# Adaptive layer-norm block on one core: the attention's output projection as two float32r matmuls on split operands, with the order of all steps remade

## The reference

```
h = layernorm(x) * (1 + ca) + sa
x = x + ga * attention(h)          # 16 query heads summed to 4, d = 16, rope, causal softmax
h = layernorm(x) * (1 + cb) + sb
x = x + gb * ffn(h)                # router; rmsnorm, wv, wo; rmsnorm, w_gate, w_up (704), w_down
```

## Time and profile before

| | us |
|---|---|
| median of 3 runs | 510.67 (510.49 to 515.2) |
| profiled execution, its own time | 510.83 |
| its span, first to last instruction | 509.1 |
| PE / PEld busy | 453.8 / 376.4 |
| DVE busy | 363.1 |
| ACT busy | 283.4 |
| POOL busy | 256.9 |

### The profile page before, as it was taken

The page is one execution under the profiler, slowest core; times in us unless marked ns, Lnnn a source line. Parts: engine busy times, 40 slices in busy tenths (PEclk is TensorE's granted clock), DMA queues, the critical chain, the costliest instruction groups (busy, mean ns, idle before and its releaser), DMA issues. The chain is left out here.

```text
span 509.1 us, 9484 instructions
## 1 busy us (share of the span) xinstructions
PE 453.8 (89%) x3308; PEld 376.4 (74%) x3308; DVE 363.1 (71%) x767; ACT 283.4 (56%) x562; POOL 256.9 (50%) x322
## 2 busy tenths in 40 slices
PE   1687879949899999699899999999999999899995
PEld 0266544738887578689887877889888688799995
DVE  4768956599999256989888444899897345847543
ACT  1066437617765684446676477556865766265340
POOL 3270056868414177657541249677524167847234
PEclk9889989968999999989999999999999999989998
DMA  7810101010010010020010010010200001001002
GB/s 226 256 27 1 22 3 42 1 48 0 2 23 1 3 42 1 2 88 2 23 52 2 3 43 1 1 47 23 85 0 8 8 1 43 1 1 42 1 1 84
DMA packets 18353, 16.07 MB, mean 32 GB/s; under 512 B 6265, under 2 KB 16958, under 8 KB 18306
## 3 DMA queue, kind: packets, MB, share of 16 engines
q1 hardware_dynamic: 18306, 15.45, 9.8%
HBM read 11.10 MB, written 4.22 MB: 30 GB/s over the span
## 5 line engine op out<-in xcount | busy, mean ns | idle before, releaser
L761 PE MATMUL banks<-gTh,guhi 128*128 128x256 f32 x352 | 103.2, 293 | 1.7 <-DVE fft L1200 1.5
L862 ACT ACTIVATE PT<-banks 128x1024 f32<-128x1024 f32 (+3 forms) x96 | 75.3, 811 | 43.9 <-PE banks L678 38.5
L763 PE MATMUL banks<-gTh,gulo 128*128 128x256 f32 x352 | 99.1, 282 | 0.0
L762 PE MATMUL banks<-gTl,guhi 128*128 128x256 f32 x352 | 99.1, 282 | 0.0
L761 PEld LDWEIGHTS banks<-gTh,guhi 128*128 128x128 f32 x352 | 66.6, 189 | 6.3 <-issue 4.6
L762 PEld LDWEIGHTS banks<-gTl,guhi 128*128 128x128 f32 x352 | 66.7, 190 | 0.3
L763 PEld LDWEIGHTS banks<-gTh,gulo 128*128 128x128 f32 x352 | 66.7, 189 | 0.0
L1111 DVE TENSOR_REDUCE mxp<-banks 128x2 f32<-128x1024 f32 (+3 forms) x56 | 61.5, 1143 | 6.2 <-PE banks L657 3.0
L516 POOL TENSOR_SCALAR_AFFINE_SELECT PT<-PT 128x512 f32<-128x512 f32 x32 | 21.2, 662 | 66.0 <-ACT PT L862 65.9
L678 PE MATMUL banks<-QKT 128*128 128x512 f32 (+3 forms) x192 | 51.9, 369 | 2.3 <-ACT PT L862 1.3
L652 PE MATMUL banks<-QKT 128*128 128x512 f32 (+3 forms) x192 | 48.8, 364 | 5.8 <-ACT QKT L842 2.1
(11 more groups left out here) (162 smaller groups left out, 1145.7 us busy)
## 6 DMA issues: line engine op xcount, KB each, us to landing
xbuf<-in_L_attn_x SPq DMA_DIRECT2D x8, 512.0 KB, 3.6
out_x<-x SPq DMA_DIRECT2D x8, 512.0 KB, 3.0
wm_st<-in_L_wmod SPq DMA_DIRECT2D x1, 1536.0 KB, 7.3
modB<-mod_scratch SPq DMA_DIRECT2D x4, 256.0 KB, 3.2
wg_st<-in_L_ffn_w_gate SPq DMA_DIRECT2D x1, 704.0 KB, 5.2
wu_st<-in_L_ffn_w_up SPq DMA_DIRECT2D x1, 704.0 KB, 6.3
x<-in_L_ffn_w_down SPq DMA_DIRECT2D x1, 640.0 KB, 5.0
QKT<-mrT SPq DMA_DIRECT2D x32, 4.0 KB
```

Source lines behind the costliest of these rows:

```text
L761: pe.matmul(out_, guhi[:, k, blk, :], gh, start=(m == 0 and k == 0), stop=False)
L762: pe.matmul(out_, guhi[:, k, blk, :], gl, start=False, stop=False)
L763: i = pe.matmul(out_, gulo[:, k, blk, :], gh, start=False, stop=(m == len(blocks) - 1 and k == KB - 1))
L862: act.activation(PT[:, u % 2, 2 * q:2 * q + 2, 0:CH - q0], both("prob", b, n)[:, :, 0:CH - q0], ACT.Exp, scale=float(D) ** -0.5).then_inc( ...
```

## The change

Both operands of the projection are split into a float32r high part and the rest. One matmul multiplies [y high; y low] (128 rows) by [Wo high; Wo high], a second one [y high; ones] (97 rows: 64 of y, and rows 64 to 96 set to one) by [Wo low; bias high; zeros; bias low]. So a `wo` step has 4 float32r matmuls in place of 4 instructions of plain float32. `ytm` gets two more DVE operations with a wait between them (a copy to float32r and a subtraction, both 128 x 256), `ynT` transposes 128 columns in place of 65, `ynev` has two ACT copies (128 x 512 and 64 x 512) in place of one, and `wob` has six DVE operations in place of one. `Wo_raw`, `Wo_b` and `mrT` now share one tile (`mrT` on partitions 96 to 103). POOL's first fill of `ytm` goes, and DVE gets two fills at the start. The stores of a chunk count on two semaphores, for even and odd batches. `ORDER` is written anew from the first word to the last.

```diff
+WB = H * D + 33
...
-ldx ldx pmod stats rstd1 norm1 norm1 xT4 setw vmod pprep0 vprep0 pprep1 stats norm1 norm1 xT3 aprep aprep aprep ldA
-wts xev qkv4 xev bias5 qkv3 aprep vprep1 gprep gprep rstd1 norm1 norm1 norm1 norm1 xT2 xT0 gprep ldB xev qkv2 xev
...
+ldx ldx pmod stats rstd1 norm1 norm1 norm1 norm1 xT4 xT5 pprep0 setw vmod vprep0 pprep1 stats rstd1 norm1 ldW wob ldA
+wts xev ldG ldG vprep1 bias3 aprep gprep norm1 norm1 norm1 aprep gprep qkv4 xev qkv5 xT2 xev aprep qkv2 xT0 xev biasq
...
-        Wo_b = sb("Wo_b", [H * D + 1, C])
+        Wo_l = sb("Wo_l", [WB, C], F32R)
+        Wo_h = sb("Wo_h", [2 * H * D, C], F32R)
...
-                        i = pe.transpose(o[0:H * D + 1, t * P:(t + 1) * P], ytm[:, t, :], ident[:])
+                        i = pe.transpose(o[:, t * P:(t + 1) * P], ytm[:, t, :], ident[:])
...
-                        i = pe.matmul(o[:, t * C:(t + 1) * C], yT65[:, (2 * n + t) % TPC, :], Wo_b[:], start=(t == 0),
+                        at = (2 * n + t) % TPC
+                        pe.matmul(o[:, t * C:(t + 1) * C], yTs[:, at, :], Wo_h[:], start=(t == 0), stop=False)
+                        i = pe.matmul(o[:, t * C:(t + 1) * C], yTo[:, at, :], Wo_l[:], start=False,
                                       stop=(t == 1))
...
-                    act.activation(yT65[:].rearrange("p t n -> p (t n)"),
-                                   of("ynT", b, n)[0:H * D + 1, :], ACT.Copy).then_inc(S["ynev"], 1)
+                    o = of("ynT", b, n)
+                    act.activation(yTs[:].rearrange("p t n -> p (t n)"), o, ACT.Copy)
+                    act.activation(yTo[0:H * D].rearrange("p t n -> p (t n)"), o[0:H * D, :], ACT.Copy
+                                   ).then_inc(S["ynev"], 1)
...
-                    dve.tensor_tensor(Wo_b[:], Wo_raw[:], Wo_b[:], ALU.mult).then_inc(S["wob"], 1)
+                    earlier("wo", NJ)
+                    y_, bias, low, high = (slice(0, H * D), slice(H * D, H * D + 1), slice(H * D, H * D + 1),
+                                           slice(WB - 1, WB))
+                    then(dve.tensor_tensor(Wo_b[:], Wo_raw[:], Wo_b[:], ALU.mult))
+                    dve.tensor_copy(Wo_h[y_], Wo_b[y_])
+                    dve.tensor_copy(Wo_h[H * D:2 * H * D], Wo_b[y_])
+                    then(dve.tensor_copy(Wo_l[high], Wo_b[bias]))
+                    dve.tensor_tensor(Wo_l[y_], Wo_b[y_], Wo_h[y_].bitcast(F32), ALU.subtract)
+                    dve.tensor_tensor(Wo_l[low], Wo_b[bias], Wo_l[high].bitcast(F32), ALU.subtract
+                                      ).then_inc(S["wob"], 1)
...
-                    dve.tensor_tensor(ytm[:, :, 0:H * D].rearrange("p t (h d) -> p t h d", h=H), o[:, :, :, 0:D],
-                                      rc[:].unsqueeze(3).to_broadcast([P, TPC, H, D]), ALU.mult
-                                      ).then_inc(S["ytm"], 1)
+                    hi, y = ytm[:, :, 0:H * D], ytm[:, :, H * D:2 * H * D]
+                    then(dve.tensor_tensor(y.rearrange("p t (h d) -> p t h d", h=H), o[:, :, :, 0:D],
+                                           rc[:].unsqueeze(3).to_broadcast([P, TPC, H, D]), ALU.mult))
+                    then(dve.tensor_copy(hi.bitcast(F32R), y))
+                    dve.tensor_tensor(y, y, hi, ALU.subtract).then_inc(S["ytm"], 1)
```

More of the change, by code:

```diff
@@ L105 @@
[L105 to L119, removed]
@@ L125 @@
[L125 to L134, removed]
@@ L140 @@
[L140 to L144, removed]
@@ L160 @@
-fflo down4 sum store store fin down5 sum down4 sum fin store
+ldx ldx pmod stats rstd1 norm1 norm1 norm1 norm1 xT4 xT5 pprep0 setw vmod vprep0 pprep1 stats rstd1 norm1 ldW wob ldA
+wts xev ldG ldG vprep1 bias3 aprep gprep norm1 norm1 norm1 aprep gprep qkv4 xev qkv5 xT2 xev aprep qkv2 xT0 xev biasq
+qkvb qkvb rope sthi qkvb aprep awd stlo qkv3 ldA wts stack0 stack4 qkvb rope stk max0 mxr stk max2 max4 mxr max6 mxr
+mxr max0 max2 sthi stlo stack6 stack4 stk max6 stk mxr max0 mxr mneg max2 mtT4 mrow max4 mxr mxr mxr mxr gprep max0
@@ new lines @@
+norm1 pv ycopy yT0 ytm rs1 rs1 norm1 a3 a6 route ynT0 ynev route had ms2 wo2 wo7 xT0 norm1 norm1 ms2 xT1 route route
+x1 x1 xev qkv0 qkvb had xev ms2 qkv1 ms2 hsel hsel rs2 rstd2 h2 rs2 qkvb rope ldx h2 ldW h2 h2 h2T0 h2hi zad rstd2
+h2T1 h2hi sthi h2lo h2lo gate7 sil stlo hsel hsel zad stats rstd1 norm1 norm1 norm1 wob stack0 stack2 gate7 stk max0
+mxr max4 stk max2 max0 xT6 sil mxr mxr mxr max4 norm1 xT7 max2 xev qkv6 up0 xev qkv7 mxr mxr qkvb mneg mtT6 gate1 mrow
+mrd up6 up2 gate3 fft ffhi sil qkvb rope sthi fft ffhi ffl sil prob4 exp fflo stlo up0 fft wts fft norm2 ffhi fflo
@@ new lines @@
+fft wts prob4 gate7 sthi exp exp store prob2 exp down6 hmod had stlo stack2 down4 hsel hsel sum ms1 ffhi ms2 prob0 stk
+max2 ffhi fflo wob zad pmask ffl mxr exp pmask sil up6 fft ms2 down5 max0 max2 pv6 mxr mxr max0 mxr rs2 h2 h2 h2T7
+h2hi h2lo max2 pv ffhi max0 mxr mxr gate7 sil stack2 stk fin sum sum prob0 fflo exp up7 fft max2 max4 mxr gate7 prob2
+exp fin pmask ffhi sil max0 mxr mxr max4 max2 hT0 mxr mxr gate1 fflo max4 prob2 mxr hhi sil hlo up7 fft pv exp prob4
+exp max2 max4 mxr up7 mxr bias0 mneg pmask pv down2 ycopy yT6 fft ffhi ffl mtT3 a1 a7 mrow ytm ynT6 rs1 route route
@@ new lines @@
+ms2 rs2 h2 hsel hsel h2 sil qkvb ytm ynT2 h2T3 up0 ynev wo2 h2hi rope rs2 h2 zad gate6 wo1 gate4 up5 x1 rstd2 fft sthi
+ffhi sil stlo h2lo fft sil fflo norm2 zad fft ffhi hmod fin ffl x1 rstd2 stack6 stack2 stk stk ffhi ms1 h2 gate0 sil
+max6 max4 mxr max2 mxr up1 ldx ldW max6 h2T4 gate0 mxr mxr fft gate5 hT1 max6 h2hi ffhi fflo fflo h2lo hhi sil max2
+mxr up4 up0 down6 rs1 stats rstd1 sil fft mxr ffhi gate4 hlo a1 fft norm2 mneg wob norm1 norm1 xT7 gate0 up5 mtT2
+norm1 norm1 ffl ffhi xev fflo sum mrow qkv7 xT2 xev sil sil gate3 qkv2 mrd hmod ldB route qkvb fft qkvb rope sil ms1
```

96 lines of the change are left out of this document (56 added, 40 removed).

## The result

The changed kernel takes 497.27 us (median of 4 runs, 495.66 to 497.57) against 510.58 before: ratio 0.9707, with 0.9643 to 0.9772 as its 95% interval. By the medians it is 13.3 us faster. (The ratio is made from all runs and isn't the quotient of the two medians, which is 0.974.) The forecast was 508.9 with a range down to 500.5, so the prediction was wrong. Of its cases rival A (500.4) comes nearest. The profiled execution took 497.57 us, its span is 495.8.

A forecast was written before the change was run, and what follows sets the result against it. PE nearly gapless from 220 us; in the first two stretches chains through DVE, ACT and DMAs end last. Span 509.1 - 2.2 + 1.5 + 0.9 - 2.1 = 507.2, plus 1.7 around it: 508.9 us; range 500.5 to 518.0.

The forecast's parts named there:

- rival A: Whole list: the old list was bad and its gaps close, PE's 4.9 us count in full; 500.4 us, chance 0.31.
- The matmuls: `wo` steps on PE: 64 matmuls go from 0.194 to 0.118 us, 4.9 us less; 3.3 us used in the sums.
- The transposes: `ynT` on PE, from 65 to 128 columns of weights: costed at nothing, 1.4 us if dearer by half.
- DVE in `ytm`: Added copy, subtraction and two waits: 0.9 us a chunk, 7 us for eight; second ACT copy 0.60 more.
- DVE in `wob`: Five more DVE operations on Wo and its bias: 1.7 us a batch, bounds 1.0 and 3.5.
- The start: `wob` ahead of `wts`: `wts` begins near 29.2, first `qkv` near 30 as before; zero, between -1 and +2 us.
- The order: Whole list: sum of the larger engine's work per stretch 420.0 to 417.8; with unchanged surplus, span 2.2 us shorter.
- +1.5 for stretch 2: Between the last `wo` of batches 0 and 1: PE and DVE, equally loaded, wait more for each other; 1.5 us added.
- +0.9 for less cover: Chains between `xT` and `down`: uncovered 3.0 us less in batches 0 and 1, 4.8 more in 2 and 3; half counted.
- The gap behind batch 0's projection stays: Between `qkv` and `stack`: 2.1 us of PE work in the new list, 1.8 before, for a chain of over 6.
- B: From `stack` to the last `mxr`, stretch 2 first: DVE becomes the bound; 523.9 us, chance 0.22.
- C: `wo` matmuls: float32r with two sources in one bank and 97 rows runs at the old pitch; 512.2 us, chance 0.04.

The follow-up runs named there:

- the bare split: Split matmuls in the old order, without y's low part, most second ACT copies and the Wo split of batches 1 to 3: 509.86 us, ratio 0.9979.
- The three hand-made lists: Kernel before, plain projection: `stlo` ahead of two `x1` (513.06 us); also `ytm` ahead of `rope` (511.7); `stlo` moved and a `wo` in bank 5 (514.29).
- The halves that don't add up: Plain projection, lists joined at batch 1's last `wo`: old then new order 501.99 us; new then old, two banks changed, 515.91 us.

## Why the prediction was wrong

*What bounds the kernel.* The sums by starts hold: 415.7 us forecast from the trace of before, and the changed list loses 78 us beside its 412.5. But I read the surplus of each stretch, 89.1 us in all, as belonging to the work of the stretch. 16 us of it belonged to the order of the steps within it, as the run with the order alone shows.

*The matmuls* were right in kind: 0.12 us apart, for 97 rows too, and 4.3 us less in all. I let 3.3 of them count in the span, 4.9 in rival A. Measured are 1.6 us in the new order, net of the late start, and 0.5, not told from nothing, in the old. There PE's waits behind 100 us sum to 24.6 us with the bare split (its profiled run is the slowest of ten) against 22.4 before, so a part of the PE work saved may have turned into waiting.

*The transposes* at nothing: a `ynT` step starts the next one 0.355 us later after, 0.401 before by the lower quartile. Right.

*DVE in `ytm`.* The two lines in the trace of after, durations in ns (min/median/max):

```profile
L1162 DVE CAST ytm<-ytm x8: 293/294/918, 83.2 to 434.6; 128x256 fp32r<-128x256 f32 x8
...
L1163 DVE TENSOR_TENSOR ytm<-ytm x8: 424/426/1451, 83.6 to 435.6; 128x256 f32<-128x256 f32 x8
```

0.28 and 0.42 were forecast. ACT has 3.6 us more, where 5 were forecast. The subtraction's 1.45 us was bounded by L1104's 1.50; that the copy can be held up as well was not priced. The chunk of batch 3 shows both beside POOL's work:

```profile
434.11 1.28 POOL L547 TENSOR_TENSOR hbuf<-hbuf,gate_b 128x512 f32<-128x512 f32 x1
434.16 0.42 DVE L1160 TENSOR_TENSOR ytm<-banks,rc 128x256 f32<-128x256 f32 x1
434.62 0.92 DVE L1162 CAST ytm<-ytm 128x256 fp32r<-128x256 f32 x1
435.47 1.28 POOL L548 TENSOR_TENSOR x<-x,hbuf 128x512 f32<-128x512 f32 x1
435.57 1.45 DVE L1163 TENSOR_TENSOR ytm<-ytm 128x256 f32<-128x256 f32 x1
436.95 0.47 DVE L1208 SCALAR_TENSOR_TENSOR hbuf<-dl,r_yes,hbuf 128x256 f32<-128x256 f32 x1
```

From the start of `yT` to that of the first `wo` of a chunk, as a mean of eight, it took 5.45 us before and 6.43 in the old order with the split projection; in the new order 5.01 with the plain one and 5.32 after. So the chain is 1.0 us longer for a chunk in the old order, where I had 0.9 for DVE and 0.6 for ACT, and 0.3 in the new, which hides most of it.

*DVE in `wob`*, 1.7 us a batch more, is a term that was mis-sized: the six operations take 2.2 us at best and 3.1 to 5.0 in the kernel after (the old one took 0.41, once 1.06), because a cast from SBUF to SBUF beside POOL is slow too (1.51, 1.33 and 1.24 us in three batches, for which I had 0.43 at most). In two batches the multiplication is as slow (1.33 and 1.51 us), with the plain projection in this order as well. So the split adds 2.7 us a batch in the new order and 2.3 in the old. The timeline of batch 3's:

```profile
350.72 0.41 DVE L1055 TENSOR_TENSOR wo_mr<-wo_mr 65x256 f32<-65x256 f32 x1
350.78 1.49 POOL L534 TENSOR_TENSOR hbuf<-hbuf,modB 128x512 f32<-128x512 f32 x1
351.17 1.24 DVE L1056 CAST Wo_h<-wo_mr 64x256 fp32r<-64x256 f32 x1
352.42 0.29 DVE L1057 CAST Wo_h<-wo_mr 64x256 fp32r<-64x256 f32 x1
352.72 0.29 DVE L1058 CAST Wo_l<-wo_mr 1x256 fp32r<-1x256 f32 x1
```

The same cast takes 1.24 us beside POOL's L534 and 0.29 behind it. The Trainium skill, "SBUF — State Buffer", section "SBUF: two separate sides", has a shared pair of ports that one of the two engines holds for an instruction; these rows fit it. Contention is at most a small part of what the new order saved, though. By the time that DVE's instructions take beyond the usual length of their kind, it is about 48 us before, 47 after, 46 with the new order alone and 50 with the projection alone.

*The start*: zero, between -1 and +2, with `wts` at 29.2. It came at 30.28 because of the 1.51 us cast, and `qkv` moved by 0.7. But the term was wrong by more than that: the first `stack` starts at 43.30 us against 40.31 before, and the new order without the split ahead of `wts` has it at 40.08. 6.8 us at the lower clock, from 31.5, lie between. 2.2 us of it are left at batch 0's last `wo`; how much reaches the end no run shows.

*The order* is the step that failed, in the sentence "With the surplus as it was, the span is 2.2 us shorter". The list alone, with everything else as before, gives 15.9 us. I carried over as a constant the one quantity that a new list exists to change. By stretches, the loss of the new order with the plain projection less that of before is +3.8, -10.4, -5.3, +0.5 and -4.8 us. Of my corrections, +1.5 for stretch 2 (two engines equally loaded) and +0.9 for less cover had the wrong sign: stretch 2 is where most came from. For the tail I gave back 2.1 of 3.7 us and it lost 4.8 less. "The gap behind batch 0's projection stays" was half right. Its waiting moved from `stack` to `gate` and fell from 5.8 to 3.4 us, but the longer part of the gain in stretch 2 came later: the steps around `ynT` of batch 1's second chunk lose 5.8 us in excess of their usual time before, most of it the wait of 3.8 us for `ytm`, and 1.8 in an `up` and a `wo` behind it at the lower clock. The new list has nothing over 0.5 us there.

My sentence in the prediction that a chain has cover or not, taken chain by chain from the list, was the wrong tool for it. The three hand-made lists show that covers can't be counted singly: a wait that is uncovered by one engine hides another one behind it, by a bank or by the next chain. The halves that don't add up show it for long parts of the list as well.

*The rivals.* A named the right mechanism, "the list was bad, and its gaps close", and was too small: it had 3.7 + 1.8 us for the gaps of the whole list and 4.9 for PE, where 15.9 and 1.6 (net of the late start) were measured. B had the mechanism of the projection's price: in the old order it gave 12.8 us more, 523.18 in all, beside B's 523.9, by DVE work that ends up on the path. That the two numbers are so near is partly luck: B has 18 us of DVE work less 4.9 of PE, the runs have 13.3 less 0.5. It didn't decide, because in the new order all but 4.4 us of it is covered, beside what batch 0's split costs. The sum 510.58 - 15.9 + 2.8 is 497.5. C is excluded by the pitch.

*What was to show it.* DVE's 377 us, the pitch, and some 58 us behind the last `wo` (55.2) came true. Stretch 2 took 110.4 us, not 121. The gap of 5 us or more ahead of batch 1's first `stack` was not there (3.4 us at the `gate` before it), and `yT` to `wo` was 0.1 us shorter and not 1.5 longer. PE's waits behind 100 us fell to 51%, where "under half" was to mean A.

## What to carry to other kernels

When a change comes with an order written anew, the order is to be judged first and by itself. The old waits are not a floor for the new list: here its order was worth over five times what the rest of the change cost. An exchange of PE work for DVE work (4.3 for 14 us here) should be measured with the order held still: it looked like part of a gain and is a loss of 2.8 us, so of the kernels run here the new order with the plain projection is the one to keep. Most of the 2.8 us are there once batch 0 is projected, behind a start that the split of Wo delays. Whether a split behind `wts` takes them back is open.

Before a single gap is closed by moving a step, look for the second wait behind the first: the bank that the step writes, and who frees it. In a list for five engines, a wait named by the profile is only the last of several. And look at the clock behind each long wait: here two long waits of PE were followed by stretches at 0.50 of full clock, so a gap cost more than its own length.

## What was not expected of the hardware

Casts from SBUF to SBUF with one input are held up beside POOL as much as subtractions: 0.29 us alone, and 0.92, 1.24 and 1.51 in the rows above. An operation on one row of 256 columns costs what one on 64 or 128 rows does (0.29 for a cast, 0.42 for a subtraction), so the two of `wob` that treat the bias alone are 0.7 us of its 2.2.
